# A transformer layer whose routed experts run only on the rows that chose them

## What is computed

```
x = x + _L0_attn_a_ref(_layernorm(x), ...)
x = x + _L0_ffn_ref(_layernorm(x), ...)
x = x + _L0_attn_b_ref(_layernorm(x), ...)
x = x + _L0_ffn_ref(_layernorm(x), ...)

_expert = silu(h @ g.T) * (h @ u.T), times d      # 128 -> 352 -> 128
probs = softmax(x @ wr.T + rb); scores, idx = top_k(probs, 2)
scores = scores / scores.sum()
out = _expert(x, shared) + sum over the 7 routed e of w[e] * _expert(x, e)
```

## Time and profile before

| | |
|---|---|
| median of 3 runs | 3311.34 us (3300.81 to 3314.95) |
| the profiled execution's own time, as the profile has it | 3301.8 us |
| its span, first to last instruction | 3301.8 us |
| PE busy | 3036.2 us, 92% |
| DVE, ACT, POOL busy | 2308.3, 1813.0, 1737.1 us |
| DMA | 139.94 MB |

### The profile page before, as it was taken

How to read it: one execution, slowest core, us unless ns; L and a number is a source line. 1 busy time by engine, 2 the same in 40 slices (tenths; PEclk the granted TensorE clock), 3 DMA queues, 4 the chain that set the end, 5 groups by cost and what they waited for, 6 DMA issues and landing times.

```text
span 3301.8 us, 87667 instructions
## 1 busy us (share of the span) xinstructions
PE 3036.2 (92%) x29986; PEld 2069.9 (63%) x29986; DVE 2308.3 (70%) x6980; ACT 1813.0 (55%) x3489; POOL 1737.1 (53%) x1382
## 2 busy tenths in 40 slices
PE   7899999999999999999999789999999999999998
PEld 4567666666666666666666456666666666666665
DVE  4568776767787677767767656766767667676667
ACT  5568666756676677667765334443434444444443
POOL 4145445544544464446444336665656666666664
PEclk7799999989999999999989779998989999998999
DMA  3011111111111111111111111111111111111111
GB/s 112 20 33 42 36 36 33 40 35 33 39 39 33 36 36 39 36 33 36 41 31 36 43 34 47 50 47 44 49 45 47 44 50 50 47 50 47 50 47 49
DMA packets 105967, 139.94 MB, mean 42 GB/s; under 512 B 13121, under 2 KB 51265, under 8 KB 105585
## 3 DMA queue, kind: packets, MB, share of 16 engines
q1 hardware_dynamic: 87408, 126.18, 12.8%
q10 hardware_dynamic: 18176, 8.92, 1.1%
HBM read 126.11 MB, written 8.95 MB: 41 GB/s over the span
## 4 chain that ended last, share of the span: by engine, by line
PE 81%; DVE 8%; issue 5%; ACT 1%; DMA 1%; POOL 1%; ACTq 0%; DVEq 0%; SPq 0%; POOLq 0%
PE bank_E L1236 13%; PE bank_E L1238 9%; PE bank_E L1237 9%; PE bank_T L1166 7%; PE bank_Y L1236 6%; PE bank_S L1157 6%; PE bank_Y L1238 4%; PE bank_Y L1237 4%; PE bank_O L1177 4%; PE bank_S L1129 3%; PE bank_O L1218 3%; PE bank_S L1138 3%; PE bank_S L1139 2%; PE bank_S L1201 1%; DVE xn L909 1%
## 5 line engine op out<-in xcount | busy, mean ns | idle before, releaser
L593 POOL TENSOR_TENSOR hid_lo<-work,hid_hi 128x512 fp32r<-128x512 f32 x660 | 841.1, 1287 | 766.4 <-ACT hid_hi L836 757.2
L725 POOL TENSOR_TENSOR work<-work 128x512 f32<-128x512 f32 x640 | 827.6, 1300 | 482.2 <-DVE work L1075 362.2
L829 ACT ACTIVATE work<-bank_E 128x512 f32<-128x512 f32 x704 | 420.1, 597 | 466.7 <-PE bank_E L1238 462.0
L1075 DVE TENSOR_TENSOR work<-work,bank_E 128x512 f32<-128x512 f32 x704 | 479.8, 683 | 170.8 <-PE bank_E L1238 75.1
L836 ACT ACTIVATE hid_hi<-work 128x512 fp32r<-128x512 f32 x704 | 441.5, 630 | 282.1 <-POOL work L725 181.9
L1068 DVE SCALAR_TENSOR_TENSOR work<-work,bank_E 128x512 f32<-128x512 f32 x704 | 480.2, 682 | 148.0 <-ACT work L829 146.2
L981 DVE CUSTOM_DVE_ANT_0 z<-bank_S,big 128x256 f32<-128x256 f32 x1024 | 390.4, 421 | 200.7 <-PE bank_T L1166 147.5
L787 ACT ACTIVATE z<-z,nm 128x256 f32<-128x256 f32 x1024 | 457.4, 501 | 40.9 <-DVE nm L981 39.0
L583 ACT COPY probT<-bank_T 128x512 f32<-128x512 f32 x512 | 296.5, 579 | 105.2 <-PE bank_T L1166 102.4
L1236 PE MATMUL bank_Y<-hid_hi,wd_hi 128*128 128x512 f32 x704 | 327.7, 465 | 24.8 <-POOL hid_lo L593 19.5
L1236 PE MATMUL bank_E<-xh,wu_hi 128*128 128x512 f32 x704 | 330.1, 469 | 1.0 <-DVE work L1068 0.8
(11 more groups left out here) (125 smaller groups left out, 4345.9 us busy)
## 6 DMA issues: line engine op xcount, KB each, us to landing
work<-wts_dram SPq DMA_DIRECT2D x224, 256.0 KB, 3.2
work<-wts_dram SPq DMA_DIRECT2D x128, 192.0 KB, 2.7
work<-wts_dram SPq DMA_DIRECT2D x128, 128.0 KB, 2.8
work<-wts_dram SPq DMA_DIRECT2D x128, 64.0 KB, 2.5
xin<-in_x SPq DMA_DIRECT2D x16, 256.0 KB, 2.8
x<-work ACTq DMA_DIRECT2D x16, 256.0 KB, 2.5
xin<-x SPq DMA_DIRECT2D x64, 64.0 KB, 1.9
out_x<-work ACTq DMA_DIRECT2D x64, 64.0 KB, 1.7
```

Of the source, the lines that this page charges most:

```text
L593: eng.tensor_tensor(hid_lo[:, n % CUT_RING, :], hid[:, n % H_RING, :], hid_hi[:, n % CUT_RING, :].bitcast(F32), ALU.subtract).then_inc(hl_ ...
L725: pool.tensor_tensor(h, h, weight[:, k % WB_RING, :], ALU.mult).then_inc(weighed, 1)
L829: act.activation(th[:, n % 2, :], product_bank(2 * n)[:, :], ACT.Tanh, scale=0.5).then_inc(th_ready, 1)
L1075: dve.tensor_tensor(hid[:, n % H_RING, :], th[:, n % 2, :], product_bank(2 * n + 1)[:, :], ALU.mult).then_inc(h_ready, 1)
```

## The change

The routed experts leave the passes. In a pass only the shared expert stays: 3 tiles of 128, 128 and 96 channels.

**In a pass,** routing gives for each row two experts and two weights. rows holds each normed row twice (POOL copies it), with its weight in column 128 and its own number in column 129, 132 numbers in all. tally counts how many earlier rows chose each expert, rank (two matmuls) gives each row its place among those, DVE turns this into the index of a row in a region of DRAM of that expert (`sent`, 7 regions), and POOL issues eight indirect transfers of 128 rows each that write them there (place). norm2 of the next pass waits for their landing before it writes rows again.

**After the last pass of a half** come the blocks. DVE makes a table from the seven totals: which expert each of 38 blocks of 512 rows belongs to, and where it begins (2 x 8192 rows are 32 full blocks, and at most 6 more). SP fills the end of each region with rows of weight 0 that point past the output. Then for each block SP loads the 512 rows, the expert's gate and up weights (704 KB) and its down weights (384 KB), which were cut at the start and stored in DRAM; PE transposes the rows, does 27 matmuls, transposes the result, ACT multiplies it by the row's weight, and POOL issues four indirect transfers that add 128 rows each to x2 or to the output in DRAM. For blocks of different experts the rows can be the same, so `add_up` waits until all earlier adds have landed. Half B begins when all adds of A have.

```diff
-                elif step == "weigh":
-                    pool.tensor_tensor(h, h, weight[:, k % WB_RING, :], ALU.mult).then_inc(weighed, 1)
+                elif step == "place":
+                    for t in range(TOK):
+                        for k in range(2):
+                            n = 2 * t + k
+                            pool.indirect_dma_start(
+                                out=sent, out_offset=bass.IndirectOffsetOnAxis(ap=slots[:, n:n + 1], axis=0),
+                                in_=rows[:, k, t, :], in_offset=None).then_inc(scattered, 16)
...
-FT = EXPERTS * INNER // P
+TILES = ((0, P), (P, 2 * P), (2 * P, INNER))
+FT = len(TILES)
+NB = 2 * MOST // BLOCK + ROUTED - 1
...
+                        if p.kind == "B" or not p.first:
+                            dve.wait_ge(scattered, p.g * (16 * 2 * TOK))
```

More of the change, by code:

```diff
@@ L154 @@
     "bturn": {"pe": 0.5, "act": 0.5}, "bout": {"pe": 0.9, "dve": 0.6}, "norm2": {"dve": 0.6},
[L156 to L160, removed]
+    "turn2": {"pe": 0.5, "act": 0.5}, "begin": {"dve": 1.0, "pe": 0.1, "pool": 0.7},
+    "logits": {"pe": 1.6, "dve": 0.3}, "route": {"dve": 0.6, "act": 0.1}, "twin": {"pool": 1.2},
+    "tally": {"pool": 1.6}, "rank": {"pe": 0.7, "dve": 0.8}, "place": {"pool": 10.0},
+    "gate": {"pe": 0.7, "act": 0.5, "dve": 0.6}, "up": {"pe": 0.7, "dve": 0.6},
+    "cut": {"act": 0.55, "pool": 1.25, "dve": 0.6},
+    "down": {"pe": 0.7}, "sum": {"act": 0.5}, "end": {"pe": 0.5, "dve": 0.6, "act": 0.1},
 }
@@ L166 @@
 RULES = {
[L167 to L172, removed]
+    "A": {"first": "longest chain", "experts": 1.0, "hand over": 0.3, "work": {}},
+    "B": {"first": "further behind", "experts": 0.97, "hand over": 0.15, "work": {}},
     "attention": {"first": "longest chain", "experts": 1.0, "hand over": 0.1, "work": {}},
-    "experts": {"first": "longest chain", "experts": 0.752, "hand over": 0.05, "work": {
-        ("act", "turn2"): 0.8, ("dve", "gate"): 0.48, ("dve", "up"): 0.32, ("pe", "turn2"): 0.27, ("pe", "up"): 0.39,
-        ("pool", "begin"): 1.44}},
+    "experts": {"first": "longest chain", "experts": 1.0, "hand over": 0.1, "work": {}},
 }
@@ L297, in steps_experts @@
     out = [("turn2", 0), ("begin", 0), ("logits", 0)]
-    out += [("route", n) for n in range(ROUTE_PARTS)] + [("wturn", 0)]
+    out += [("route", n) for n in range(ROUTE_PARTS)] + [("twin", 0), ("tally", 0), ("rank", 0), ("place", 0)]
     for i in range(FT):
-        out += [("gate", i), ("up", i), ("weigh", i), ("cut", i), ("down", i)]
+        out += [("gate", i), ("up", i), ("cut", i), ("down", i)]
     return out + [("sum", 0), ("end", 0)]
@@ L385, with run_passes @@
 EXPERTS_ALONE = order("A", [], steps_experts())
-def run_passes(engine, name, attention, experts, before=lambda: None, after=lambda: None):
+def run_passes(engine, name, attention, experts, blocks, before=lambda: None, after=lambda: None):
     def run(steps, this, following, ahead):
@@ L1296 @@
+            run_passes(pe, "pe", attention, experts, blocks)
 def kernel(**inputs):
@@ L1305, with weights @@
     b_b = a("attn_b_qkv_bias").reshape(P, 3)
[L1307 removed]
+    def weights(g, u, d):
+        down = np.zeros((DN, D), np.float32)
+        down[:INNER] = d.T
+        return np.concatenate([g.T, u.T, down.reshape(FT, P, D).transpose(1, 0, 2).reshape(P, DN)], 1)
+    experts = [(a("ffn_sg"), a("ffn_su"), a("ffn_sd"))]
+    experts += [(a("ffn_rg")[e], a("ffn_ru")[e], a("ffn_rd")[e]) for e in range(ROUTED)]
     arrays = {
```

708 lines of the change are left out of this document (511 added, 197 removed).

## The result

The changed kernel took 3783.95 us (median of 4 runs, 3766.87 to 3798.72) against 3308.01 of the kernel before: 1.145 times as long, 95% interval 1.140 to 1.149. The forecast was 3204 us. The profiled execution's span is 3775.7 us, its own time 3777.49. Of all executions behind the times in this document one fell in the chip's slower state, the second of e10 (3812 us), and it is left out.

The account below looks back on a forecast made before the run. TensorE was taken as the bound. Start 121.2, A passes 1,380, between halves 415, B attention 52.3, B passes 825 and end 401 made 3,194.5, plus 9.5: 3204 us; own range 3090 to 3320, wider range 2960 to 3440.

Parts of the forecast that it names:

- I let these cancel: A pass: added products and delays offset by a higher clock and less POOL interference, leaving 92 us.
- the 91.7 us of attention alone: A pass: attention with no experts beside it and without bias flips, at clock 0.66 in the units.
- My upper end of 105: A pass: units at 2.44 us (1.2 GHz), 12.7 + 78.1 + 9.6 + 5.
- rival 4: Both passes shrink less: A 103, B 62, 270 us more, total 3474; chance 0.08.
- The B pass at 55: B pass: 52.3 us alone; 27 products (11.6) and some 4 more fall mostly in PE's gaps.
- my upper end of 62: B pass: upper end of the estimate of 55 us, whose lower end was 45.
- Hidden behind these: Passes: added routing work, including eight scatters at 1.3 us (10.4 on POOL), costs no pass time.
- The block at 9.1: Blocks: each period takes 9.1 us, set by DVE's written order; 76 blocks make 692 us.
- the sum over DVE's order: Blocks: DVE's operations and waits for ACT in sequence, 8.35 to 8.6, with handovers 9.0 us.
- 4t + L = 8.4: Blocks: POOL's four adds at t = 1.3 plus landing L = 3.2, just under the 9.1 period.
- Rival 1: Blocks: the chain of adds decides if t exceeds 1.48 or L 3.9; period 11.2, total 3364; chance 0.20.
- Rival 2: Blocks: the clock falls to 1.2 GHz, PE needs 13.3 us a block, total 3523; chance 0.10.

Follow-up runs that it names:

- e10: Changed kernel with six places instead of four in the ring of rows, and 44 extra matmuls in A passes: 3719 us.
- e1: Changed kernel without the eight scatters of each pass; blocks read and add to the spare rows: 3573 us.
- e4: Changed kernel without the four adding transfers of each block: 3614 us.
- e5: Changed kernel with the low cut of a block's first tile moved from POOL to VectorE: 3601 us on chip 1.
- e8: Changed kernel with 60 extra full matmuls into an unused bank per A pass, gate and up on two banks instead of three: 3441 us on chip 1.
- e6: Changed kernel with odd blocks adding to a second DRAM buffer with its own semaphore, left out of the result: 3546 us.
- e15: The kernel of e8 again, on chip 4 beside the changed kernel: 3675 us.

## Why the prediction was wrong

- **"I let these cancel"** is the step that failed. In it the experts' dense matmuls held the clock up for some of the units, which was to pay for the 27 products and the rest beside the 91.7 us of attention alone, and so the A pass was 92. In fact the remaining 27 products do not hold the clock up: 0.63 over the whole pass. The price is 17.7 us a pass, 266 us. Of these, 3 to 4 go with the scatters (e1 against e4, 105.9 against 109.0). The other 14 are the added work, which nothing paid for: 91.7, with the clock of 0.66 that it had alone, plus 27 products at the lower clock (27 x 0.43 = 11.6) and 2 for the rest make 105.3, and without the stutter the pass took 105.9 (e1, e5). That it hangs on the clock e8 shows: 60 full matmuls put in gave 12.2 of the 14 back, their own time paid (105.9 to 93.7). My upper end of 105 was that case, and too low by the stutter alone; rival 4, which named it, had 0.08 and said 103. The clock of 0.66 stood in my own rows; I had no row in which 27 products raised it.
- **The B pass at 55** took the low clock into account, yet was 13.5 short: 9.1 are the stutter beside the scatters (59.4 without, which is inside my upper end of 62), the other 4.4 were not traced further. "Hidden behind these" was the step: POOL had time for the scatters, but what went with them on PE, 89.6 us of waiting in the rows of bank O alone, was not in the sum.
- **The block at 9.1**: the sum over DVE's order was good; e4 without adds has 8.8. The term that failed is the adds' loop, "4t + L = 8.4". t with the gap of 0.30 is 1.86 instead of 1.3; L was right (3.2 assumed, 3.2 found): 10.6. Rival 1's mechanism, with its "t over 1.48", decided in the blocks, 1.5 us each, 115 us in all. Its reason was not right: the issue is dear by itself, not by meeting VectorE. Over all 304 adds the shortest took 1.557 us, the median 1.56, the longest 2.09. The Trainium skill (SBUF — State Buffer, the box on DVE blocking DMA) says that GpSimd cannot write a transfer's descriptors while VectorE runs an operation in a 2-port mode; by the page's figure I had estimated a period near 15 us, and no transfer here shows a wait of that size. And one limit was missing from all my rivals: the ring of four rows, which still holds the block at 10.4 when POOL's wait for landing is gone (e6).
- **Rival 2** (the clock falls in the blocks) was rightly small: 0.98.
- **What held:** the start (118.8 against 121.2), B attention alone, the shape of a half around its blocks, and no wait for the expert weights.
- Three misses had one sign and added up: 266 + 203 + 115 of 581. The range treated them as nearly independent.

No version beat the kernel before. The best that computes all is e8: 3441 us on chip 1 (1.038 times before), 3675 on chip 4 as e15 (1.114).

## What to carry to other kernels

When dense matmuls are taken out from beside small ones, price what stays at the clock that it had alone, not at the clock that it had beside them, and add what runs beside it at that clock too; here a removal of 40 us of work (an estimate, 171 x 0.235) gave 1.9. Where two waits could each explain the period, remove them singly and together: singly each looked innocent. When an edit that cannot touch a stage seems to speed it, run the unedited kernel on the same chip before believing either.

## What the runs showed of the hardware that was not expected

- TensorE busy 83% of the time by the profile, in the main with transposes, 32-row scores and 32-column mixes, was granted 0.63 of its clock; with one 128x512 matmul before each unit and 28 in the head, 0.93 (e8) and 0.90 (e15).
- The profile's busy share did not tell the clock: in the blocks it was 75% (276.70 of 370.80 us) at a clock of 0.98, in the A passes 83% at 0.63, in e8's A passes 90% at 0.93. The Trainium skill (TensorE: Matmul & The Clock Gate, What's actually happening) says that a monitor sets the clock by how busy PE has been recently; in these rows the clock does not follow the profile's busy share.
- An indirect transfer of 128 rows occupies GpSimd 0.96 us when it stores and 1.56 us when it adds, with 0.30 between two.
- While GpSimd issued eight storing ones, PE stood still again and again, for 0.4 to 1.2 us in the rows above, without a wait that the trace shows (66 matmuls instead of 155 in 9.9 us). B passes were longer by this on three of four chips and in the first profile (68.0 to 71.3 us without extra matmuls in them), and not on the fourth (58 to 61); the VectorE and ScalarE work that hangs on PE came late with it.
- Two low cuts that met, one on VectorE and one on GpSimd, took 2.44 and 1.88 us instead of 0.69 and 1.29.
